# Two graph layers on one core: bias and norm vectors loaded as rows, x in halves, batch 0's bias on PE, new program orders

## The reference

```python
u = x @ x.T / sqrt(128);  s = softmax(u) * adj;  att = s / (rowsum(s) + 1e-10)
ctx = upper(att) @ (x Wl.T + bl) + diag(att) @ (x Ws.T + bs) + lower(att) @ (x Wr.T + br)
o   = relu(ln_w * (ctx - mean) / sqrt(var + 1e-12) + ln_b)
x1  = layernorm(x + o)
d   = (rowsum(adj) + 1e-5) ** -0.5
out = layernorm(x1 + (d * adj * d.T) @ x1 @ W1 + b1)
```

## Time and profile before

| | before |
|---|---|
| median of 3 runs | 462.99 us |
| runs | 461.92 to 464.63 us |
| the profiled execution, span from first to last instruction | 461.6 us |
| PE busy | 444.2 us (96%) |
| DVE busy | 388.8 us (84%) |
| ACT busy | 296.8 us (64%) |
| POOL busy | 310.9 us (67%) |
| DMA | 79.9 MB, mean 173 GB/s |

### The profile page before, as it was taken

One profiled execution on the slowest core, in us unless ns is written; L12 is line 12 of the kernel. 1 busy time (PEld: TensorE's weight loads), 2 busy tenths in 40 slices (PEclk: granted clock), 3 DMA queues, 4 the chain that ended last, 5 costly groups with the idle time before them and its releaser, 6 DMA issues. The chain is left out here.

```text
span 461.6 us, 8799 instructions
## 1 busy us (share of the span) xinstructions
PE 444.2 (96%) x2663; PEld 357.7 (77%) x2663; DVE 388.8 (84%) x696; ACT 296.8 (64%) x611; POOL 310.9 (67%) x364
## 2 busy tenths in 40 slices
PE   6899999999999999999999999999999999999974
PEld 4689879589776988679786797769887697879453
DVE  2998899979999889988899889998899887988625
ACT  2768767666666766765767657676676667677320
POOL 2115767379758867588675886588675967889662
PEclk9999999999999999999999999999999999999988
DMA  5836758285773889259881779528893493367721
GB/s 176 288 139 176 236 132 266 58 210 182 168 225 95 207 259 243 83 143 260 201 241 39 186 229 227 189 74 212 253 220 129 120 240 127 69 161 175 176 62 45
DMA packets 68878, 79.88 MB, mean 173 GB/s; under 512 B 7232, under 2 KB 60608, under 8 KB 68832
## 3 DMA queue, kind: packets, MB, share of 16 engines
q1 hardware_dynamic: 68768, 79.26, 62.1%
q0 software_dynamic: 64, 0.07, 0.0%
HBM read 38.40 MB, written 4.19 MB: 92 GB/s over the span
## 5 line engine op out<-in xcount | busy, mean ns | idle before, releaser
L478 PE MATMUL ps_c<-h_sum,dT 128*128 128x128 f32 x896 | 110.5, 275 | 0.9 <-issue 0.9
L478 PEld LDWEIGHTS ps_c<-h_sum,dT 128*128 128x128 f32 x896 | 106.9, 192 | 4.6 <-issue 4.0
L1405 POOL TENSOR_TENSOR dM<-dT,parts 128x384 f32<-128x384 f32 x64 | 67.9, 1063 | 58.2 <-ACT junk_d L826 31.7
L498 PE MATMUL ps_y<-aT,x1p 128*128 128x512 f32 x224 | 104.3, 592 | 0.0
L805 ACT ACTIVATE d_rows<-ps_u,nmax 128x1024 f32<-128x1024 f32 x62 | 68.9, 1112 | 50.3 <-DVE nmax L1060 50.2
L812 ACT ACTIVATE dT<-ps_d 128x1024 f32<-128x1024 f32 x64 | 65.3, 1021 | 40.8 <-PE ps_d L463 35.1
L1060 DVE TENSOR_REDUCE nmax<-ps_u 128x1 f32<-128x1024 f32 x62 | 75.3, 1215 | 16.6 <-PE ps_u L405 15.8
L1067 DVE CUSTOM_DVE_ANT_0 d_rows<-d_rows,a_rows 128x1024 f32<-128x1024 f32 x64 | 84.8, 1326 | 0.4 <-ACT d_rows L805 0.4
L1074 DVE STREAM_TRANSPOSE a_blk<-a_rows 128x1024 f32<-128x1024 f32 x64 | 77.4, 1228 | 0.8 <-DMA a_rows<-in_adj_dram 0.8
L818 ACT ACTIVATE junk<-a_rows 128x1024 bf16<-128x1024 f32 x64 | 67.1, 1048 | 0.3
L463 PE MATMUL ps_d<-parts,d_rows 128*128 128x128 f32 x512 | 66.4, 273 | 0.0
(11 more groups left out here) (95 smaller groups left out, 692.1 us busy)
## 6 DMA issues: line engine op xcount, KB each, us to landing
a_rows<-in_adj_dram SPq DMA_DIRECT2D x64, 512.0 KB, 4.5
aT<-a_blk SPq DMA_DIRECT2D x224, 128.0 KB, 2.9
x_rows<-in_x_dram SPq DMA_DIRECT2D x8, 512.0 KB, 4.5
a_rows<-a_blk SPq DMA_DIRECT2D x32, 128.0 KB, 2.4
out_dram<-fin SPq DMA_DIRECT2D x15, 256.0 KB, 2.6
x_turned<-x_blk SPq DMA_DIRECT2D x96, 32.0 KB, 1.9
out_dram<-fin SPq DMA_DIRECT2D x2, 128.0 KB, 1.8
fin<-in_L_gnn_Wl_dram SPq DMA_DIRECT2D x1, 64.0 KB, 3.4
```

Source lines behind the costliest of these rows:

```text
L478: pe.matmul(ps_c[:, c_place(b, i), :], dT[:, i % 2, j, :], h_sum[:, b % 2, j, k * H:(k + 1) * H], start=t == 0, stop=False)
L498: last = pe.matmul(y_bank(b, i0, i1), gathered(b)[:, j, :], turned(b)[:, i0:i1, :, j, :].rearrange("p i q c -> p (i q) c"), start=j == 0, ...
L1405: pool.tensor_tensor(dM[:, i % 2, :, :], dT[:, i % 2, i, :].rearrange("p (a c) -> p a c", a=1).to_broadcast([P, 3, P]), parts[:, :, :], AL ...
```

## The change

Five things. (1) The three biases and the three vectors ln_w, ln_b, b1 are loaded as plain rows of 512 bytes into partition 0 of `c_rows`. PE spreads each group of three over 128 partitions with a product of a row of ones with the row (`spread(0)`, `spread(1)`, 384 columns, one contraction row, float32, into `ps_m`), and ACT copies each out (`spread_copy`) into `vectors_bc`. (2) In batch 0 each `project` gets a fourth product, ones by bias row, and ACT copies the bank to `h_sum` (`h_out`, 384 columns) where DVE's `add_bias` stood; from batch 1 on it is as before. (3) x of batch 0 is loaded in two halves, with the three weight DMAs between them, and the weights are transposed before the second half of x. (4) POOL writes the row of ones. (5) The call lists of all engines and of SP are new in every part; also the cut between `first_batches`, `batch` and `last_batches` lies elsewhere (the middle function now begins with the last third of the batch before, `scores(p, 6)` among it), which moves no work. In `batch`, per batch, the same calls are made as before.

What the prediction speaks of beside the lines shown: on ACT in batch 0 the order is h_out(0), h_out(1), exps(0), degree(0), h_out(2), exps(1), h_out(3), d_out(0), h_out(4), degree(1), exps(2), h_out(5), d_out(1), exps(3), h_out(6), exps(4), h_out(7). On PE in the middle batches: scores(b, 4), m_read_h(b, 6), project(b, 7), turn_d(b, 2), context_far(b, 0), context_near(b, 0), context_far(b, 1), scores(b, 5), context_near(b, 1), turn_d(b, 3), context_far(b, 2), gather(p, 0, HB, 4, 5). On PE in the last batch project(b, 7), scores(b, 4), turn_d(b, 2), context_far(b, 0) as before. On DVE there: row_max(b, 3), add_bias(b, 6), masked(b, 2), add_bias(b, 7), turn_blocks(b, 2), row_max(b, 4), masked(b, 3). On SP in the last batch: move_blocks(p, 1), store, load_a(b, 7), move_blocks(b, 0), move_blocks(b, 1), the stores.

The diff, cut to its core:

```diff
         wT_lo = sb("wT_lo", [P, 3 * H], F32R)
-        bias_bc = sb("bias_bc", [P, 3 * H])
+        vectors_bc = sb("vectors_bc", [P, 2, 3 * H])
+        bias_bc = vectors_bc[:, 0, :]
+        lnw_bc, lnb_bc, b1_bc = (vectors_bc[:, 1, k * H:(k + 1) * H] for k in range(3))
         w1_sb = sb("w1_sb", [P, H])
-        lnw_bc = sb("lnw_bc", [P, H])
-        lnb_bc = sb("lnb_bc", [P, H])
-        b1_bc = sb("b1_bc", [P, H])
 
         x_rows = sb("x_rows", [P, 2, NB, H])
         xT_hi = sb("xT_hi", [P, 2, N], F32R)
...
+        vectors = c_rows[0:1, 0:6, :].rearrange("o k h -> o (k h)")
+        ones_row = c_rows[0:1, 6, :]
...
         def add_bias_on(eng, b, j):
-            if b == 0 and j == 0:
-                eng.wait_ge(bias_in, 48)
+            eng.wait_ge(spread_out, 1)
             wait(eng, ctx_done, NB * (b - 1))
             eng.wait_ge(h_ready, NB * b + j + 1)
-            eng.tensor_tensor(h_sum[:, b % 2, j, :], ps_m[:, 0:3 * H], bias_bc[:, :], ALU.add).then_inc(h_added, 1)
+            eng.tensor_tensor(h_sum[:, b % 2, j, :], ps_m[:, 0:3 * H], bias_bc, ALU.add).then_inc(h_added, 1)
...
+            def load_x_half(b, half):
+                sp.dma_start(x_rows[:, b, blocks_of(half), :], x_block_rows(x, b, HALF * half, HALF * (half + 1)))\
+                  .then_inc(x_in[b] if half else x0_in, 16)
...
-            def load_biases():
-                for k, v in enumerate((bl, br, bs)):
-                    sp.dma_start(bias_bc[:, k * H:(k + 1) * H], v.partition_broadcast(P)).then_inc(bias_in, 16)
-
-            def load_norm_constants():
-                for t, v in ((lnw_bc, ln_w), (lnb_bc, ln_b), (b1_bc, b1)):
-                    sp.dma_start(t[:, :], v.partition_broadcast(P)).then_inc(bcast_in, 16)
+            def load_vectors(half):
+                for k, v in enumerate((ln_w, ln_b, b1) if half else (bl, br, bs)):
+                    sp.dma_start(c_rows[0:1, 3 * half + k, :], v.rearrange("(o h) -> o h", o=1))\
+                      .then_inc(vector_in[half], 16)
...
             def first_batches(b, p):
 
-                load_x(p)
+                load_x_half(p, 0)
                 load_weights()
-                load_biases()
+                load_x_half(p, 1)
+                load_vectors(0)
                 load_a(p, 0)
                 load_a(p, 1)
-                load_norm_constants()
-                load_a(p, 2)
-                next_x(p)
-                load_a(p, 3)
-                next_a(p, 0)
-                load_a(p, 4)
+                load_vectors(1)
+                load_a(p, 7)
                 load_a(p, 5)
                 load_a(p, 6)
-                next_a(p, 1)
-                load_a(p, 7)
-                next_a(p, 2)
+                load_a(p, 2)
+                load_x(b)
+                load_a(p, 3)
+                load_a(b, 1)
+                load_a(p, 4)
+                load_a(b, 4)
+                load_a(b, 3)
+                load_a(b, 0)
+                load_a(b, 2)
                 move_blocks(p, 0)
...
 
             def turn_x(b, k):
-                pe.wait_ge(x_in[b % 2], 16)
+                pe.wait_ge(x0_in if b == 0 and k == 0 else x_in[b % 2], 16)
                 for j in range(HB):
                     last = pe.transpose(x_columns(b, k)[:, j * P:(j + 1) * P], x_rows[:, b % 2, HB * k + j, :], ident)
                 last.then_inc(xt_tr, 1)
@@ -450,8 +456,16 @@
                 if b == 0 and j == 0:
                     pe.wait_ge(const_ok, 1)
                 s = slice(j * P, (j + 1) * P)
-                split_matmul(ps_m[:, 0:3 * H], xT_hi[:, b % 2, s], xT_lo[:, b % 2, s], wT_hi[:, :], wT_lo[:, :])\
-                    .then_inc(h_ready, 1)
+                last = split_matmul(ps_m[:, 0:3 * H], xT_hi[:, b % 2, s], xT_lo[:, b % 2, s], wT_hi[:, :], wT_lo[:, :], b > 0)
+                if b == 0:
+                    pe.wait_ge(vector_in[0], 48)
+                    last = pe.matmul(ps_m[:, 0:3 * H], ones_row, vectors[:, 0:3 * H], start=False, stop=True)
+                last.then_inc(h_ready, 1)
+
+            def spread(half):
+                pe.wait_ge(vector_in[half], 48)
+                pe.matmul(ps_m[:, 0:3 * H], ones_row, vectors[:, 3 * H * half:3 * H * (half + 1)],
+                          start=True, stop=True).then_inc(spread_made, 1)
 
...
 
                 turn_x(p, 0)
+                turn_weights()
                 turn_x(p, 1)
-                turn_weights()
                 m_read_x(p, 0)
                 project(p, 0)
                 scores(p, 0)
@@ -525,16 +539,16 @@
                 m_read_h(p, 1)
                 project(p, 2)
                 scores(p, 2)
-                scores(p, 3)
-                turn_d(p, 0)
                 m_read_h(p, 2)
                 project(p, 3)
-                scores(p, 4)
+                turn_d(p, 0)
                 m_read_h(p, 3)
                 project(p, 4)
-                turn_d(p, 1)
+                scores(p, 3)
                 m_read_h(p, 4)
                 project(p, 5)
+                turn_d(p, 1)
+                scores(p, 4)
                 m_read_h(p, 5)
                 project(p, 6)
                 turn_d(p, 2)
@@ -542,101 +556,166 @@
                 project(p, 7)
                 scores(p, 5)
                 m_read_h(p, 7)
-                turn_x(b, 0)
+                spread(0)
                 context_far(p, 0)
                 context_near(p, 0)
                 context_far(p, 1)
+                m_read_s(0)
+                spread(1)
+                context_near(p, 1)
                 scores(p, 6)
-                context_near(p, 1)
                 turn_d(p, 3)
+                m_read_s(1)
+                turn_x(b, 0)
                 context_far(p, 2)
...
                 context_far(b, 3)
                 context_near(b, 3)
                 scores(b, 6)
+                gather(p, 0, HB, HB, 5)
                 turn_d(b, 5)
-                gather(p, 0, HB, 4, 6)
-                gather(p, 0, HB, 6, 8)
+                gather(p, 0, HB, 5, NB)
+                context_far(b, 4)
                 scores(b, 7)
-                context_far(b, 4)
                 m_read_h(b, 7)
                 second_product(p, 0, HB)
+                turn_d(b, 6)
                 context_near(b, 4)
-                turn_d(b, 6)
+                context_far(b, 5)
                 gather(p, HB, NB, 0, 1)
-                context_far(b, 5)
+                turn_d(b, 7)
                 gather(p, HB, NB, 1, 2)
-                turn_d(b, 7)
                 context_near(b, 5)
+                gather(p, HB, NB, 2, 3)
                 context_far(b, 6)
+                gather(p, HB, NB, 3, 7)
                 context_near(b, 6)
+                gather(p, HB, NB, 7, NB)
                 context_far(b, 7)
                 context_near(b, 7)
-                gather(p, HB, NB, 2, 4)
-                gather(p, HB, NB, 4, 6)
-                gather(p, HB, NB, 6, 8)
                 m_read_o(p, 0, HB)
                 second_product(p, HB, NB)
-                gather(b, 0, HB, 0, 4)
-                gather(b, HB, NB - 2, 0, 2)
+                gather(b, 0, HB, 0, 1)
+                gather(b, HB, NB - 2, 0, 1)
+                gather(b, 0, HB, 1, 3)
                 gather(b, NB - 2, NB, 0, 2)
-                gather(b, 0, HB, 4, 6)
-                gather(b, 0, HB, 6, 8)
-                gather(b, HB, NB - 2, 2, 3)
+                gather(b, 0, HB, 3, HB)
+                gather(b, NB - 2, NB, 2, 3)
+                gather(b, HB, NB - 2, 1, HB)
+                gather(b, NB - 2, NB, 3, HB)
+                gather(b, HB, NB - 2, HB, 5)
+                gather(b, 0, HB, HB, NB - 2)
+                gather(b, HB, NB - 2, 5, NB - 2)
+                gather(b, 0, HB, NB - 2, NB)
+                gather(b, NB - 2, NB, HB, 5)
+                gather(b, HB, NB - 2, NB - 2, 7)
                 m_read_o(p, HB, NB)
...
@@ -797,6 +817,14 @@
                 act.activation(x_half(xT_hi, b, k), x_columns(b, k), ACT.Copy, scale=SHRINK)\
                    .then_inc(xt_hi, 1)
 
+            def spread_copy(half):
+                act.wait_ge(spread_made, half + 1)
+                act.activation(vectors_bc[:, half, :], ps_m[:, 0:3 * H], ACT.Copy).then_inc(spread_out, 1)
+
+            def h_out(j):
+                act.wait_ge(h_ready, j + 1)
+                act.activation(h_sum[:, 0, j, :], ps_m[:, 0:3 * H], ACT.Copy).then_inc(h_added, 1)
+
...
                 weights()
                 x_low(p, 1)
-                add_bias(p, 0)
+                row_max(p, 0)
                 turn_blocks(p, 0)
-                row_max(p, 0)
-                add_bias(p, 1)
                 row_max(p, 1)
                 masked(p, 0)
+                masked(p, 1)
+                turn_blocks(p, 1)
                 row_max(p, 2)
-                add_bias(p, 2)
                 row_max(p, 3)
-                add_bias(p, 3)
-                masked(p, 1)
-                add_bias(p, 4)
                 masked(p, 2)
```

(47 more changed lines are left out.)

773 lines of the change are left out of this document (392 added, 381 removed).

## The result

The change makes the kernel slower by a third of a per cent: 464.42 us (median of 15 runs, 463.97 to 466.0) against 463.34 us for the kernel before on the same chip (15 runs, 461.92 to 466.01), ratio 1.0033 [1.0019, 1.0048]. The profiled execution spans 462.5 us, before 461.6. The forecast was 461.4 us: the sign was wrong, though the result lies inside the forecast's whole range and inside the 0.5% that was called the same.

What follows compares the result with a forecast made beforehand. PE's own work was taken to bound the middle, with room only at the two ends. The terms summed to -1.6 us on a span of 461.6, giving 460.0; the median adds 1.4, so 461.4 us, range 456.5 to 467.0.

Steps and rivals of the forecast that it cites:

- bias products: Ten float32 products of 384 columns on PE, eight in batch 0 and two spreads, 0.65 us each: +6.5 us.
- waits of batch 0: PE's waits for DVE's `add_bias` to empty the bank go: 4.4 us less 0.8 left, -3.6 us.
- start: First `project` waits for the weights' low part; weights ahead of half of x gain little: -0.1 us.
- spreads' round trips: `ps_m` must be copied out after each spread before PE writes it again, nearly covered by other work: +0.3 us.
- `context_far(b, 0)` of the last batch: PE's wait of 0.92 us there, for an `add_bias` behind two `masked` on DVE, goes: -0.9 us.
- tail before PE's end: Last batch: four PE waits and the low clock, 6.3 us in all, go except 0.7 us: -5.6 us.
- tail behind it: Behind PE's last product, two earlier `norm_f` now precede the last one on DVE: +1.3 us, bounds 0.4 to 2.
- middle batches: Before `gather` product 4, `masked(b, 3)` and an `add_bias` ahead of `stats_x` may stall PE: 0.1 a batch, +0.5 us.
- rival (A): The bias product is cheap, one row takes 0.17 us: 4.8 us less, 456.6 us; chance 0.18.
- Rival (B): Batch 0: PE waits for ACT's `h_out` as it did for `add_bias`; 3.6 us not won, 465.0 us; chance 0.10.
- (D): Middle batches: `masked(b, 3)` ahead of `stats_x` stalls PE 1.3 us at `gather` product 4 each, 467.4 us; chance 0.16.
- Rival (C): Tail keeps its DMA wait and lower clock, as `masked(b, 7)` or `degree(b, 7)` ends late: 465.5 us; chance 0.08.

Runs made afterwards that it cites:

- e2: Changed kernel with the bias and spread products at 128 contraction rows, 127 of them zero: 460.63 us, ratio 0.9937.
- e3: Changed kernel with the bias and spread products at 32 contraction rows, 31 of them zero: 464.43 us, ratio 1.0027.
- e1: Changed kernel without the fourth product of each `project` in batch 0, biases left out there: 458.88 us, ratio 0.99.
- e6: Changed kernel with `d_out(b, 1)` ahead of `norm_c` on ACT in the middle batches: 468.75 us, ratio 1.0126.
- e4: Changed kernel with `stats_x` ahead of `masked(b, 3)` on DVE in the middle batches, as before the change: 464.25 us, ratio 1.0032.
- e16: Kernel before with the new lists only from the end of `batch(6, 5)` on, and three order edits at the handover: 460.57 us, ratio 0.9942.
- e7: Changed kernel with the last batch's `turn_blocks` 4 to 7 put back to late places on DVE: 472.6 us, ratio 1.0192.
- e8: Changed kernel with batch 0's old lists, biases spread by loads and added by DVE, later orders new: 468.19 us, ratio 1.0112.
- e11: Kernel before with the new lists of all engines only from the end of `batch(6, 5)` on: 466.97 us, ratio 1.0078.
- e12: Changed kernel with full-height float32r bias and spread products and the old order of the middle batches, last batches new: 468.71 us, ratio 1.0105.

## Why the prediction was wrong

| term | forecast | measured (gaps by starts) |
|---|---|---|
| bias products | +6.5 | +10.4 |
| waits of batch 0 | -3.6 | -6.2 |
| start | -0.1 | 0 |
| spreads' round trips | +0.3 | 0 |
| `context_far(b, 0)` of the last batch (370 to 400 us) | -0.9 | -0.9 |
| tail before PE's end | -5.6 | -5.3 |
| tail behind it | +1.3 | +1.2 |
| middle batches | +0.5 | +1.7 |
| sum | -1.6 | +0.9 |

The miss of 2.5 us is +3.9 from the bias products and +1.2 from the middle, less 2.6 that the waits of batch 0 gave beyond the forecast. The forecast missed by little only because larger errors stood against each other. With the bias products priced right and all else as it was, it would have been +2.3 us, the right sign.

**The step that failed is the price of the bias product.** It was put at 0.65 us from rows of 128 contraction rows, with 0.17 and 0.89 as bounds; it measured 1.04, outside both. The size by columns and type was right (e2: 0.65), and what was missing is that a product lower than the array costs 0.39 more, with one row as with 32 (e3). The upper bound was no bound: a full product of more columns does not bound a lower one. The page of the Trainium skill that the prediction cited (TensorE: Matmul & The Clock Gate, Why this matters for your kernels) has a single product over 32 rows cost what one over 128 does; for a product among full-height ones the measurement decides against it, 1.04 against 0.65. No run here has such a product by itself. It did point the right way, against rival (A), which is out.

**The waits of batch 0** were worth more than the profile's wait rows say: 3.7 us in rows, 4.4 with the drains as I scaled them, 6.2 by starts, since short gaps of 0.1 to 0.3 us around each wait have no row. Nothing was left of them, because the longer bias products gave DVE and ACT the time; e1 shows it from the other side, where 8.3 us of products out gave only 5.1. Rival (B) is out.

**The middle** was under-sized. The stall of 0.31 us at `gather` product 4 and 0.23 before `turn_d(b, 2)` make 0.54 a batch; smaller gaps of the kernel before went, and 0.3 is left. (D)'s mechanism, a chain without slack there, is shown by e6. Its cause, `masked(b, 3)` ahead of `stats_x`, holds `stats_x` back by 0.9 us, as the starts in e4 show; that e4 gained nothing is `power_x` beside `masked`. (D)'s price of 1.3 us a batch was not reached, since the chain from `stats_x` to x1p took 6.09 us (130.76 to 136.85) and not its earlier 6.84 (179.25 to 186.09).

**The tail** came out as summed, e16 bears it out, and its main reason holds: with `turn_blocks` ahead of `masked(b, 7)` the moves end 4.4 us earlier in e16, where over 4.9 was forecast. In the kernel after this is hidden, since PE, `masked(7, 7)` and the moves all run later there. Rival (C) was right that `masked(b, 7)` now releases the moves (it ends at 427.18, the first of them is issued at 427.26), and wrong that the wait stays. e7 shows the other side, though its low clock followed another wait.

Of what should have shown it: waits on `h_out` below 1 us, no idle on the last moves, clock of 1.00 while PE works and a late last `norm_f` came true; PE busy rose by 6.9 where 6 was forecast; records of 0.33 us (0.53) and no stall before `gather` product 4 (0.31) did not come true.

## What to carry to other kernels

Give a product with few contraction rows the array's full height by rows of zeros, and float32r parts where the value can be split: here 1.04, 0.65 and 0.19 us for the same sum. Price an instruction form that the trace does not hold by a run of its own, or widen the bounds past the neighbours. Treat a hand-written order as fitted at its joints: all three orders that were first spliced here (e8, e11, e12) lost over 4 us at one handover, each time to an `x_low` behind work that could wait. Judge whether a transfer comes earlier by how far its user has got, not by the clock: here both had moved.

## What the runs showed of the hardware

A float32 product of 384 columns among full-height ones takes 1.04 us with 1 or with 32 contraction rows and 0.65 with 128; a fifth of the 1.04 lies in the neighbours' starts and not in its own records. The bounds here are 32 and 128 rows; nothing between them was run.

VectorE's `masked`, with two inputs in SBUF, and GpSimd's `power_x` side by side: `power_x` took 1.97 us in five of five batches (e4), and 1.02 where they don't meet.

Behind a wait of PE the granted clock fell to 0.50, the lower level, in the kernel before (2.24 us, then 0.50 from 442 to 444), in e7 (2.50 us, the same stretch) and in e11 and e8 (4.3 us; 0.50 from 380 to 384 and from 42 to 46). Behind the wait of 2.25 us in e7, and behind those of 0.7 and 0.35 us in e16, it stayed at 1.00.
